# Router choices of an expert layer stored without their zeros, loaded two pairs at a time and padded on GpSimd, with a running maximum in the router

## The reference

```
grouped = x.reshape(B, g, t, d)                      # groups of t = 32 tokens, g = 256 of them
logits = jnp.einsum('bgtd,des->bgtes', grouped, controller)
tie = jnp.linspace(0.0, 1e-06, t).reshape(t, 1, 1)
logits = logits + tie
perm = (logits == jnp.max(logits, axis=-3, keepdims=True)).astype(x.dtype)
dispatched = jnp.einsum('bgtd,bgtes->bgesd', grouped, perm)
inner = relu(jnp.einsum('bgesd,desf->bgesf', dispatched, f1) + bias)
intermediate = jnp.einsum('bgesf,esfd->bgesd', inner, f2)
out = jnp.einsum('bgesd,bgtes->bgtd', intermediate, perm)
```

## Time and profile before

| what | us |
|---|---|
| median of three runs | 2271.55 (2269.86 to 2272.39) |
| the profiled execution | 2268.97 |
| its span, first to last instruction | 2267.2 |
| PE (TensorE matmuls) busy | 1907.8 (84%) |
| DVE (VectorE) busy | 1399.9 (62%) |
| ACT (ScalarE) busy | 940.6 (41%) |
| POOL (GpSimd) busy | 437.6 (19%) |

### The profile page before, as it was taken

How to read it: one execution, slowest core, us unless ns; L and a number is a source line. 1 busy time by engine, 2 the same in 40 slices (tenths; PEclk the granted TensorE clock), 3 DMA queues, 4 the chain that set the end, 5 groups by cost and what they waited for, 6 DMA issues and landing times. The chain is left out here.

```text
span 2267.2 us, 34624 instructions
## 1 busy us (share of the span) xinstructions
PE 1907.8 (84%) x12342; PEld 1295.5 (57%) x12342; DVE 1399.9 (62%) x2708; ACT 940.6 (41%) x1763; POOL 437.6 (19%) x282
## 2 busy tenths in 40 slices
PE   7999999999998799999889999994667675576444
PEld 6777777777776444444378888883536352352000
DVE  5887778777778454555468888874434354363344
ACT  4444444444444344544345554552323232242222
POOL 1100100010000144554355555530000000000000
PEclk9999999999999899999989999995888888697655
DMA  5233333333332588888688887758797999999999
GB/s 164 75 117 125 112 111 111 132 112 103 115 134 90 180 224 234 221 220 222 168 259 251 246 245 224 251 161 282 258 397 277 391 349 409 402 327 410 372 391 339
DMA packets 306366, 522.10 MB, mean 230 GB/s; under 512 B 27119, under 2 KB 126485, under 8 KB 297877
## 3 DMA queue, kind: packets, MB, share of 16 engines
q1 hardware_dynamic: 296981, 503.11, 66.3%
q10 hardware_dynamic: 9216, 16.78, 1.9%
HBM read 313.98 MB, written 205.82 MB: 229 GB/s over the span
## 5 line engine op out<-in xcount | busy, mean ns | idle before, releaser
L89 PE MATMUL p_pu<-p_xT_high,p_win_high 128*128 128x512 f32 (+1 forms) x816 | 329.4, 404 | 14.6 <-DVE p_win_low L84 12.3
L90 PE MATMUL p_pu<-p_xT_high,p_win_low 128*128 128x512 f32 (+1 forms) x816 | 312.8, 383 | 0.0
L91 PE MATMUL p_pu<-p_xT_low,p_win_high 128*128 128x512 f32 (+1 forms) x816 | 312.4, 383 | 0.0
L444 ACT ACTIVATE p_t<-p_pu,p_tbias,p_taps 128x512 f32<-128x512 f32 (+1 forms) x192 | 146.7, 764 | 357.9 <-PE p_pu L91 357.1
L561 DVE SCALAR_TENSOR_TENSOR p_t<-p_pu,p_taps,p_t 128x256 f32<-128x256 f32 (+1 forms) x384 | 208.5, 543 | 6.9
L839 POOL TENSOR_TENSOR q_y<-q_y 128x512 f32<-128x512 f32 x128 | 160.4, 1271 | 190.2 <-DVE q_y L860 190.2
L84 POOL TENSOR_TENSOR p_xT_low<-p_xT,p_xT_high 128x2048 fp32r<-128x2048 f32 (+1 forms) x16 | 71.3, 4454 | 617.6 <-ACT p_xT_high L79 617.6
L89 PEld LDWEIGHTS p_pu<-p_xT_high,p_win_high 128*128 128x128 f32 x816 | 154.9, 190 | 47.1 <-DVE p_xT_low L84 9.9
L91 PEld LDWEIGHTS p_pu<-p_xT_low,p_win_high 128*128 128x128 f32 x816 | 154.3, 189 | 32.8
L90 PEld LDWEIGHTS p_pu<-p_xT_high,p_win_low 128*128 128x128 f32 x816 | 154.9, 190 | 25.4
L1439 PE MATMUL e_pd<-e_taken,e_ff 128*32 128x128 f32 x2048 | 85.5, 321 | 99.1 <-DMA e_ff<-in_L_ffn_f 95.4
(11 more groups left out here) (127 smaller groups left out, 3720.3 us busy)
## 6 DMA issues: line engine op xcount, KB each, us to landing
...
s_SV<-p_sout SPq DMA_DIRECT2D x128, 256.0 KB, 2.0
q_av<-s_SV SPq DMA_DIRECT2D x64, 512.0 KB, 4.3
s_Z<-q_z SPq DMA_DIRECT2D x128, 256.0 KB, 3.2
o_zin<-s_Z SPq DMA_DIRECT2D x64, 512.0 KB, 3.9
e_ff<-in_L_ffn_f SPq DMA_DIRECT2D x64, 512.0 KB, 8.5
...
e_taken<-s_I SPq DMA_DIRECT2D x32, 1024.0 KB, 11.4
```

What stands on the lines that cost most here:

```text
L89: pe.matmul(out, a[0], b[0], start=start, stop=False)
L90: pe.matmul(out, a[1], b[0], start=False, stop=False)
L91: return pe.matmul(out, a[0], b[1], start=False, stop=stop)
L444: nc.scalar.activation(t[r][m % 2][:, c], pu[(W + n) % 3][:, c], ACT.Identity, bias=tbias[:, w:w + 1], scale=taps[:, w, 2:3]).then_inc(t_o ...
```

## The change

The choices are stored once, without the zeros. TOOK becomes a tensor of half the size, with the two halves of the expert sets outermost, then partition, tile and expert set; a store holds a unit (eight tiles), so that each partition writes rows of 2 KB. ScalarE copies the first half unit, VectorE the second, and there are two buffers `o_took` of a unit each in place of four of half a unit. In the experts phase a load `e_picked` brings the choices of four tiles (two pairs, 128 KB) into one of three buffers, in rows of 1 KB; GpSimd makes the padded choices of a pair from it with two products by the columns of `side`, into one of two buffers `e_pick`, for which TensorE waits. The small table `side` is loaded at the start of the experts phase. In the router the maximum over the 32 tokens isn't taken in one reduction per unit any more; VectorE keeps a running maximum per half (`o_top`), one operation behind each write of logits, and `choose` only compares.

```diff
@@ output_phase @@
-    NZ, NR, NK = 3, 6, 4
+    NZ, NR, NK = 3, 6, 2
-        top = [sb(f"top{s}", [P, UG]) for s in range(2)]
-        took = [sb(f"took{s}", [P, 4, 2, 2, ES // 2]) for s in range(NK)]
+        top = [sb(f"top{s}", [P, N1]) for s in range(2)]
+        took = [sb(f"took{s}", [P, 2, 8, ES // 2]) for s in range(NK)]
                 for b in range(2):
-                    v = 2 * u + b
-                    for s in range(2):
-                        sp.wait_ge(took_ok[s], ONE + v + 1)
-                    sp.dma_start(td[v], took[v % NK][:].rearrange("p b h g e -> p b (h g e)")).then_inc(took_st[v % NK], 16)
+                    sp.wait_ge(took_ok[b], ONE + u + 1)
+                sp.dma_start(S["TOOK"][:, :, 8 * u:8 * u + 8, :].rearrange("h p m e -> p h (m e)"),
+                             took[u % NK][:].rearrange("p h m e -> p h (m e)")).then_inc(took_st[u % NK], 16)
+        def keep_took(eng, copy, v):
+
+            u, b = v // 2, v % 2
+            eng.wait_ge(t_ps, ONE + v + 1)
+            if u >= NK:
+                eng.wait_ge(took_st[u % NK], ONE + u // NK * 16)
+            copy(took[u % NK][:, :, 4 * b:4 * b + 4].rearrange("p h m e -> p m h e"),
+                 pt[b][:].rearrange("p m (h e) -> p m h e", h=2)).then_inc(took_ok[b], 1)
             def keep_logits(n):
+                best, now = top[n // HALF], logit[:, :, n // HALF, n % HALF]
                 dve.wait_ge(l_ps, ONE + n // 2 + 1)
-                dve.tensor_scalar(logit[:, :, n // HALF, n % HALF], pl[:, n % 2], float(tie[n % HALF]), None, ALU.add
-                                  ).then_inc(l_ok, 1)
+                dve.tensor_scalar(now, pl[:, n % 2], float(tie[n % HALF]), None, ALU.add).then_inc(l_ok, 1)
+                dve.wait_ge(l_ok, ONE + n + 1)
+                if n % HALF:
+                    dve.wait_ge(top_ok, ONE + n)
+                    dve.tensor_tensor(best[:], best[:], now, ALU.max).then_inc(top_ok, 1)
+                else:
+                    dve.tensor_copy(best[:], now).then_inc(top_ok, 1)
             def choose(u):
-                dve.wait_ge(l_ok, ONE + (half + 1) * HALF)
-                dve.tensor_reduce(top[u % 2][:], by_group, AX.X, ALU.max).then_inc(top_ok, 1)
-                dve.wait_ge(top_ok, ONE + u + 1)
+                dve.wait_ge(top_ok, ONE + (half + 1) * HALF)
                 dve.tensor_tensor(by_group, by_group,
-                                  top[u % 2][:].rearrange("p (g a) -> p g a", a=1).to_broadcast([P, UG, GT]),
+                                  top[half][:, g:g + UG].rearrange("p (g a) -> p g a", a=1).to_broadcast([P, UG, GT]),
                                   ALU.is_equal).then_inc(take_ok, 1)
@@ experts_phase @@
-    NP = 4
+    NP, NK = 2, 3
+    NW = TH // 4
             def load_picks(w):
-                if w >= STEPS * PH:
+                if w >= STEPS * NW:
                     return
-                c, j = w // PH, w % PH
-                if w >= NP:
-                    sp.wait_ge(tile_ps, ONE + (w - NP + 1) * 2)
-                sp.dma_start(pick[w % NP][:], td[(c // 2) * PH + j, c % 2]).then_inc(pick_in[w % NP], 16)
+                c, q = w // NW, w % NW
+                if w >= NK:
+                    sp.wait_ge(pick_ok, ONE + (w - NK + 1) * 2)
+                at = (c // 2) * TH + 4 * q
+                sp.dma_start(picked[w % NK][:], S["TOOK"][c % 2, :, at:at + 4, :]).then_inc(picked_in[w % NK], 16)
-            for j in range(2):
-                load_pair(0, j)
+            for j in range(NK):
                 load_picks(j)
+                if j < 2:
+                    load_pair(0, j)
-                    load_picks(c * PH + j + NP)
+                    if j % 2:
+                        load_picks(c * NW + j // 2 + NK)
         @block.gpsimd
         def _(pool):
             nc.gpsimd.memset(eps[:], EPS).then_inc(eps_ok, 1)
+            pool.wait_ge(consts, ONE + 32)
+            for n in range(STEPS * PH):
+                w = n // 2
+                pool.wait_ge(picked_in[w % NK], ONE + (w // NK + 1) * 16)
+                if n >= NP:
+                    pool.wait_ge(tile_ps, ONE + (n - NP + 1) * 2)
+                for g in range(2):
+                    x = pool.tensor_scalar(pick[n % NP][:, :, g * EH:(g + 1) * EH], picked[w % NK][:, n % 2 * 2:n % 2 * 2 + 2, :],
+                                           side[:, g:g + 1], None, ALU.mult)
+                x.then_inc(pick_ok, 1)
             def dispatch(c, j):
-                pe.wait_ge(pick_in[(c * PH + j) % NP], ONE + ((c * PH + j) // NP + 1) * 16)
+                pe.wait_ge(pick_ok, ONE + c * PH + j + 1)
```

49 lines of the change are left out of this document (16 added, 33 removed).

## The result

The changed kernel takes 2251.11 us (median of 4 runs, 2247.88 to 2252.09), against 2271.32 for the one before on the same chip: a ratio of 0.991, with a 95% interval of 0.9896 to 0.9924. It is faster, by 20.2 us where 25.4 were forecast; the profiled run took 2251.35 us, its span is 2249.6. Where the 17.6 us of span went is read from the starts of TensorE's matmuls in the two timelines. Each stretch ends where the next begins; "loop" is the first o_pc matmul to the first transpose of choices, "tail" from there to the first dispatch. A dispatch runs from its first matmul to the first of the layers behind it, "layers" from there to the next dispatch.

The account below looks back on a forecast made before the run. TensorE bounds the output phase, the DMA the tail and steps 2 and 3. Terms 11.8 + 0 - 0.4 + 3 + 4 + 7 = 25.4 off 2268.97 give 2243.6, 2246 at the median's level; range 2231 to 2259.

Parts of the forecast that it names:

- Tail: Stores behind the router loop: 4.19 MB fewer at a full DMA's 355 GB/s gain 11.8 us, bounds 8 and 14.5.
- the start: Start of the experts phase: one small load (side) issued ahead costs 0.4 us, bounds 0 and 2.
- Rival D: Stores and loads of TOOK: the new layout moves at 171 GB/s, all is given back, 2272 us; chance 0.02.
- Running maximum: Router loop: VectorE's 0.8 us more for two tiles fits in its 0.87 us wait for TensorE; cost 0.
- Rival C: Router loop: the slack doesn't hold; at 1.2 us for two tiles 9 us go, 2255 us; chance 0.18.
- Rival F: Router loop: the maximum meets GpSimd's product in every pair of tiles, 27 us back, 2273 us; chance 0.02.
- Padding: Dispatches: GpSimd's 128 operations at 0.5 us, 1.3 a pair with hand-over, lie beside the pair between; cost 0.
- rival E: Dispatches: GpSimd becomes the bound; slower begins at 1.2 us an operation, 2289 us at 1.7; chance 0.08.
- Step 0: First dispatch: the first gap shrinks and moves to pair 6, the second shrinks; 3 us gained, bounds 1 and 11.4.
- Step 1: Second dispatch: the 2.59 us gap shrinks to about 1.3, smaller ones go; 4 us gained, bounds 2 and 5.
- Steps 2 and 3: Last two dispatches: each reads 1.05 MB in place of 2.10 on a full DMA; 7 us gained, bounds 5 and 10.
- Layers: Expert layers: bound by weights and stores, which the change leaves alone, so what is won before them passes through.

Follow-up runs that it names:

- second profile: The changed kernel run once more with no edit; 2248.54 us, ratio 0.9901 to the kernel before.
- pad_twice: The changed kernel with GpSimd making each padded pair twice; 2260.2 us, ratio 0.9954 to the kernel before.
- before_first: The kernel before the change, with pick loads ahead of their turn's pair load and the four weight transfers one turn later; 2265.72 us, ratio 0.9968.
- picks_short: The changed kernel with each pick load bringing two tiles of choices instead of four, both pairs using these; 2242.68 us, ratio 0.9879 to the kernel before.

## Why the prediction was right, and where it was off

**Tail: 11.8 forecast, less 0.4 for the start; 12.5 measured (12.3 in the second profile).** The step held: the bytes left out, at the rate of a full DMA. From the start of the last writes of logits (1531.32 before, 1534.49 after) the full stretch ended after 39.2 us, now after 25.9: 13.3 gained. The same 8.39 MB at 388 in place of 355 GB/s are 2.0 us of that, within the bound that I kept for longer rows; the start of the experts phase took 0.9 back where I had 0.4. Rival D, memory that takes the 16 KB pitch badly, is out: 380 to 395 GB/s.

**Running maximum: 0 forecast, 1.3 us measured, 2.2 with its part of the tail.** The price was right (0.74 for two tiles against 0.8 estimated), the cover of 0.87 too, but "it fits by a hair: cost 0" was not. VectorE's wait is not all there is to cover: ScalarE hands on what VectorE is late with, and o_xT comes 0.10 us ahead of the logits in place of 0.84. Rival C is right in kind, at a fraction of its 9 us, but its sign, gaps of TensorE before y_low, was the wrong place to look. The gain "below 2" in the steps with a selection is 0.7. Rival F, the meeting with GpSimd's product, did not come: L1164 takes 0.37 to 0.40 us in all its 62 instructions.

**Padding: 0 forecast.** An operation takes 0.602 us (0.5 taken, 0.26 to 1.05 as bounds). pad_twice shows the point from which it decides: a pair's own time, as rival E had it. Beyond that a pair takes the whole of GpSimd's time, 2.44 us, and not half of a sum (2.3 by E's formula). Rival E is out.

**Step 0: 3 forecast, 1.6 and 2.3 measured.** Issue and landing of the load for pair 6 came as reckoned: pair 6 starts 16.96 us after the first dispatch matmul, where the forecast (1597 by the clock of before) had 17.0. The failed step is the second gap: "a gap of 4 to 5 in place of 5.2" was 6.1 and 5.6. Its load is issued only after pair 9, behind four weight loads, as the load of pair 13 was. TensorE has one pair more left to run (10 to 13, where it had 10 to 12), some 1.4 to 1.8 us. But the landing takes 9.7 us in place of 9.3, and from the landing to the pair it is now 1.4 us (1608.67 to 1610.03), with the padding and the hand-over, where it was 0.1. These take back what the one pair more gave.

**Step 1: 4 forecast, 1.9 and 2.6 measured.** What I reckoned came, and something else took half of it. From the start of pair 2 on, the dispatch shrank from 35.3 to 31.5 us, 3.8; but pair 2 itself starts 12.7 us after the first matmul where it was 10.8. Its X stands in a full DMA queue behind the last stores and weights of the layers, and the windows at that place are at a share of 0.98 to 1.05 in both kernels. I had not followed the landing of pair 2, the wait that is next in line. That it is the change's doing is not shown: this wait is 6.1 to 9.9 us over the fourteen profiles, and 8.5 in before_first.

**Steps 2 and 3: 7 forecast, 7.0 measured (9.8 in the second profile).** That the size came out is in part luck. Dispatch 2 moves 2.1 MB less, which at its 370 GB/s is 5.7 of its 6.0 us, but the picks are only half of that; the other half is what layers 1 moves more. Layers 1 and dispatch 2 together are 3.5 us shorter for 1.1 MB, which is what the forecast had for one step; dispatch 3 gained 1.0 (2.9 in the second profile) and layers 2 lost 1.1. Inside dispatch 2 the waits for picks fell from 7.4 to 3.7 us in sum, other waits grew by 1.5, and the rest is matmuls at a granted clock of 0.91 in place of 0.81.

**Layers: 0 forecast, 3.2 us lost in sum over rows 0 to 2.** "What is won before them passes through" failed for layers 1: 63.6 and 64.4 us against 61.1. The matmuls are the same (512 of the first layer) and their waits for weights 4 us longer, 19.4 against 15.3 us. Those waits are not the whole of it, since picks_short has 19.3 us of them too and takes 60.1 us. What goes with the time is the megabyte more: the kernels with 22.8 MB or more in layers 1 take 62.8 to 64.5 us, those with 21.7 to 22.3 take 60.1 to 62.7. So the loss reads as a part of dispatch 2's gain, moved over the border between the two; no run was made to test that. Why it moves in some kernels and not in others stays open.

In all: forecast 2246, measured 2251. In the profiled run 7.8 us are missing: 1.7 ahead of the loop (scatter at least in part), 1.6 in the loop, 1.4 in step 0, 2.1 in step 1 and 3.2 in the layers, less 1.1 each that the tail and the last combine gave beyond their terms.
